# Merged turns of a decoder kernel: row maxima ahead of the eviction of the projections, and the feed-forward's products ahead of turned scores and head outputs

## What is computed

```
h = _layernorm(x, ln1_s, ln1_b)
q, k, v = h @ Wq + bq, h @ Wk + bk, h @ Wv + bv
qp = elu(q) + 1.0;  kp = elu(k) + 1.0
kv = einsum('bshd,bshm->bhmd', kp, v);  ksum = sum(kp, axis=1)
z = 1.0 / (einsum('blhd,bhd->blh', qp, ksum) + EPS_ATTN)
x = x + (einsum('blhd,bhmd,blh->blhm', qp, kv, z) @ Wo + bo)
x = x + relu(_layernorm(x, ln2_s, ln2_b) @ W1 + b1) @ W2 + b2
```

```
scores = einsum('bhqd,bhkd->bhqk', q, k) / sqrt(D_HEAD)
_, idx = top_k(scores, TOP_K)
attn = einsum('bhqk,bhkd->bhqd', softmax(where(kept, scores, -inf)), v)
return x + attn @ w_out_w.T + w_out_b
```

## Time and profile before

| | us |
|---|---|
| median of 3 runs | 1457.76 |
| lowest and highest | 1451.19, 1458.03 |
| the profiled execution | 1452.29 |
| its span | 1450.5 |
| TensorE busy, share of the span | 1045.4, 72% |
| VectorE | 998.1, 69% |
| ScalarE | 670.8, 46% |
| GpSimd | 478.6, 33% |

### The profile page before, as it was taken

The page is one execution under the profiler, slowest core; times in us unless marked ns, Lnnn a source line. Parts: engine busy times, 40 slices in busy tenths (PEclk is TensorE's granted clock), DMA queues, the critical chain, the costliest instruction groups (busy, mean ns, idle before and its releaser), DMA issues.

```text
span 1450.5 us, 17894 instructions
## 1 busy us (share of the span) xinstructions
PE 1045.4 (72%) x5082; PEld 692.4 (48%) x5082; DVE 998.1 (69%) x3106; ACT 670.8 (46%) x1767; POOL 478.6 (33%) x468
## 2 busy tenths in 40 slices
PE   3887764555466727777584669878899883988999
PEld 2676642323244515555362334333344452766787
DVE  5666668878547778777876876753867858765332
ACT  2444425733166515665413754335776653633322
POOL 4233335602244413444522730033433423221100
PEclk9989976866677858887655889989999895889999
DMA  4100010000000000000001001101111120222343
GB/s 124 30 13 25 29 50 0 1 0 1 0 13 17 14 1 26 5 17 9 1 1 51 1 1 53 50 22 48 51 45 45 47 74 15 74 70 92 113 136 122
DMA packets 41106, 53.88 MB, mean 37 GB/s; under 512 B 6112, under 2 KB 20080, under 8 KB 41008
## 3 DMA queue, kind: packets, MB, share of 16 engines
q1 hardware_dynamic: 40336, 50.80, 11.5%
q0 software_dynamic: 672, 1.98, 0.4%
HBM read 51.71 MB, written 1.05 MB: 36 GB/s over the span
## 4 chain that ended last, share of the span: by engine, by line
PE 42%; DVE 24%; ACT 7%; issue 6%; POOL 5%; DVEq 1%; POOLq 0%; ACTq 0%
PE psum L1663 7%; PE psum L1674 6%; PE psum L1649 6%; PE psum L1406 2%; PE psum L1430 2%; PE psum L1524 2%; PE psum L1388 2%; POOL Wk L680 2%; PE psum L1336 2%; PE psum L1258 2%; PE psum L1478 2%; DVE S L2461 2%; DVE smax L2466 2%; ACT far L988 2%; DVE nmax L2045 1%
## 5 line engine op out<-in xcount | busy, mean ns | idle before, releaser
L2173 DVE TENSOR_TENSOR big<-psum,qe 128x512 f32<-128x512 f32 x106 | 72.9, 688 | 157.5 <-PE psum L1674 75.5
L1134 ACT ACTIVATE qe<-psum 128x512 f32<-128x512 f32 x106 | 62.3, 595 | 127.6 <-PE psum L1663 127.5
L1649 PE MATMUL psum<-big,wexp 128*128 128x256 f32 (+1 forms) x340 | 117.8, 462 | 0.0
L988 ACT ACTIVATE far<-far,half_far,fmul 128x128 bf16<-128x128 bf16 x256 | 102.9, 488 | 22.5 <-DVE hit L1948 22.5
L637 POOL TENSOR_SCALAR veps<-mv 128x4 f32<-128x4 f32 x34 | 8.3, 244 | 291.0 <-DVE mv L1868 291.0
L1961 DVE MAX8 near<-Wk 128x8 f32<-128x128 f32 x512 | 103.0, 275 | 0.0
L735 POOL TENSOR_TENSOR Wk<-Wk,far 128x1024 f32<-128x1024 f32 x32 | 68.2, 2134 | 67.2 <-ACT far L988 67.2
L1258 PE MATMUL psum<-ident,h 128*128 128x128 f32 x172 | 37.5, 347 | 71.0 <-DVE h L1875 47.7
L1649 PEld LDWEIGHTS psum<-big,wexp 128*128 128x128 f32 x340 | 70.0, 206 | 30.5 <-issue 21.9
L1875 DVE TENSOR_SCALAR h<-xs,mv,rstd 128x128 f32<-128x128 f32 x128 | 53.1, 478 | 41.3 <-POOL rstd L639 38.1
L1336 PE MATMUL psum<-ident,Wk 128*128 128x128 f32 x256 | 45.7, 344 | 49.1 <-POOL Wk L680 45.4
(11 more groups left out here) (344 smaller groups left out, 2898.2 us busy)
## 6 DMA issues: line engine op xcount, KB each, us to landing
wexp<-in_mg SPq DMA_DIRECT2D x48, 256.0 KB, 2.6
wexp<-in_mu SPq DMA_DIRECT2D x48, 256.0 KB, 2.9
wexp<-in_md SPq DMA_DIRECT2D x48, 256.0 KB, 3.0
w<-in_aw SPq DMA_DIRECT2D x8, 256.0 KB, 2.9
w<-in_w2a SPq DMA_DIRECT2D x8, 256.0 KB, 2.5
wqkv<-in_aw SPq DMA_DIRECT2D x8, 192.0 KB, 2.2
ctxt<-in_ctx SPq DMA_DIRECT2D x5, 256.0 KB, 5.2
xin<-in_x SPq DMA_DIRECT2D x4, 256.0 KB, 3.0
```

The source lines that it names most:

```text
L988: ins = act.activation(far[t][:, hd, :], far[t][:, hd, :], ACT.Identity, bias=half_far[:, 0:1], scale=fmul[t][:, hd:hd + 1])
L1649: mm = pe.matmul(bank(4)[:, 0:w], wd[l % 2][:, c + j, :], hid_of[k >= EARLY][k % CH][:, j * w:(j + 1) * w], start=first and j == 0, stop=l ...
L2173: dve.tensor_tensor(hid_of[k >= EARLY][k % CH], bank(U_BANK[k]), sg_of[k >= EARLY][k % 2], ALU.mult).then_inc(hu_done, 1)
```

## The change

Four engines have a `merged_turn`; three of them are rewritten, in order alone. No instruction is added or taken away.

- DVE: `maxima(b)` stood between the unsettled check of `b - 1` and its branch; it now stands ahead of `head_outputs` and of the eviction of the projections.
- PE: `turned_maxima` ahead of `sums`; `feed(b, 0)` ahead of the first half of the turned scores; `feed(b, 1)` ahead of the second half; the first two quads of head outputs behind `down`, the last two behind `output`.
- ACT: the copy of the feed-forward's input ahead of the spread maxima; the first two hidden chunks ahead of the first exponential.

```
@@ ACT, merged_turn @@
+                if fed:
+                    feed(b, "input")
                 if 0 <= b - 1 < NB:
                     maxima(b - 1)
-                if fed:
-                    feed(b, "input")
                 if here:
                     penalties(b, range(0, 6))
+                if fed:
+                    feed(b, 0)
                 if old:
                     exponentials(b - 2, 0)
-                if fed:
-                    feed(b, 0)
                 if here:
                     penalties(b, range(6, 11))
                 if old:
@@ PE, merged_turn @@
                     feed(b, "input")
+                if before:
+                    turned_maxima(b - 1)
                 if step:
                     attend(b + 1, "sums")
-                if before:
-                    turned_maxima(b - 1)
+                if fed:
+                    feed(b, 0)
                 if old:
                     turned_scores(b - 2, 0)
-                if fed:
-                    feed(b, 0)
                 if step:
                     attend(b + 1, "attention")
-                if old:
-                    turned_scores(b - 2, 1)
                 if fed:
                     feed(b, 1)
                 if old:
-                    outputs(b - 2, 0)
-                    outputs(b - 2, 1)
+                    turned_scores(b - 2, 1)
                 if step:
                     attend(b + 1, "attended")
                 if fed:
                     feed(b, "down")
                 if old:
+                    outputs(b - 2, 0)
+                    outputs(b - 2, 1)
+                if step:
+                    attend(b + 1, "output")
+                if old:
                     outputs(b - 2, 2)
                     outputs(b - 2, 3)
-                if step:
-                    attend(b + 1, "output")
@@ DVE, merged_turn @@
                     step_normalize("F", b + 1)
+                if here:
+                    maxima(b)
                 if old:
                     head_outputs(b - 2)
                 if after:
                     attend(b + 2, "projections")
                 if before:
                     unsettled_rows(b - 1)
-                if here:
-                    maxima(b)
-                if before:
                     settle(b - 1)
```

## The result

The changed kernel took 1476.95 us (median of 4 runs, 1475.96 to 1481.94) against 1457.89 for the kernel before, measured beside it: a ratio of **1.0149, 95% interval 1.0126 to 1.0173**, some 22 us slower by that ratio (19 between the medians). The profiled execution took 1477.58 us with a span of 1475.8, against 1452.29 and 1450.5; the second is one of the shorter ones of the kernel before, so the 25.3 us between the two spans are more than the measured loss. The forecast was 1461 and its range ended at 1472: the direction of its sum was right, its size was not.

What follows compares the result with a forecast made beforehand. No engine is full in a turn; a chain across engines, mainly VectorE and TensorE, bounds it. Turn 1's 1.4 plus 5 x 1.0 gave +6.4 us on 1454.6, so 1461 us, range 1448 to 1472.

Steps and rivals of the forecast that it cites:

- Early maxima, bare branch: Row maxima moved ahead of the eviction leave the settled branch bare (some 1.55 us); keys come 0.73 earlier, at +4.10.
- Hold by GpSimd: GpSimd's product starts earlier, beside VectorE's queries in turns 2 to 6, holding them near 4 us; masked sums end at +12.62.
- the value for turn 1: In turn 1 the keys are held by GpSimd's product: +1.4 us, between -1.4 and +2.4, the latter if queries late too.
- Head outputs behind `down`, 1.69: On TensorE, 1.69 us of head outputs comes after down, ahead of output projection and scores, in turns 2 to 6.
- The clock is worth 0.2 here, not 1.8: Ahead of attention in turns 2 to 6: a higher clock ends turned scores at +10.99, but attention waits for masked sums, +12.62.
- So I charge nothing for the clock: The gap ahead of down, two pieces under 1 us, shorter than the 1.31 before the second scores, costs no clock.
- a sign of a falling clock: Down products taking well above 4 us, over 5 instead of 3.57, would show the clock falling ahead of them.
- The rival of a clock falling in the new gap: Clock falls in the wait ahead of down: up to 2.0 us in five turns, +16.4 in all, 1471; chance 0.24.

Runs made afterwards that it cites:

- e3: The changed kernel, but GpSimd starts its product of scores and signs only when the positive queries are done: 1462.89 us, ratio 1.0050 to the kernel before.
- e13: The kernel before, with two groups of head outputs (narrow products) computed a second time behind down in turns 2 to 6: 1486.10 us, ratio 1.0197.
- e14: The kernel before, with eight wide 128x128 products added behind down in turns 2 to 6: 1473.53 us, ratio 1.0115.
- e9: The changed kernel, with the first two groups of head outputs also computed ahead of down, filling TensorE's idle time: 1482.19 us, ratio 1.0153 to the kernel before.
- e7: The changed kernel with the edits of e3, e4 and e5 together: 1440.75 us, ratio 0.9895 to the kernel before.
- e4: The changed kernel, but ScalarE evicts up products 2 and 3 ahead of the second exponential: 1469.09 us, ratio 1.0095 to the kernel before.
- e5: The changed kernel with the move of the head outputs undone, the first two groups again ahead of down: 1455.16 us, ratio 0.9998 to the kernel before.
- e6: The changed kernel with the edits of e3 and e4 together: 1447.48 us, ratio 0.9953 to the kernel before.

## Why the prediction was wrong

By its own steps:

- *Early maxima, bare branch: right.* Forecast keys at +4.10, measured +3.82 in turn 4, where the branch showed 1.24 bare, not 1.55; in turn 2 it showed 1.89 and the keys came at +4.48.
- *Hold by GpSimd: right, and the value for turn 1 too small.* L2267 took 4.09 in turn 4, masked sums ended at +12.34 (forecast +12.62); with GpSimd's product behind the queries (e3) it took 0.68. The Trainium skill (SBUF — State Buffer, SBUF: two separate sides) has the ports that the two engines share as an exclusive lock, and the trace agrees: the held queries ended 0.54 behind GpSimd's product. In turn 1 the forecast was +1.4 with a bound of +2.4. Keys and queries were both held (3.16 and 1.75), which made `at` 2.3 late and the turn 3.3 longer; e13 and e14, which change nothing in turn 1, had 34.62 and 35.01 there, so between 2.2 and 3.3 of it is the change. The bound, not the value, was near.
- *Head outputs behind `down`, 1.69: right.* From the start of `down` to first scores it took 8.11 in turn 4 against 6.34 before.
- *"The clock is worth 0.2 here, not 1.8": wrong.* I had let TensorE arrive early, wait for the masked sums and then go on at the upper level. In turn 4 it waited 3.23 and then took 4.56 for attention and the second up products instead of 2.75; `down` started at +21.30, 1.5 behind the forecast +19.80, which the clock's 1.8 covers. e3 takes the wait away, and there the same products take 2.85 in turn 4. I had given the clock its worth where it rises, and not asked what the wait that it makes does next.
- *"So I charge nothing for the clock": wrong, and the step that failed.* I had compared the gap ahead of `down` with one of 1.31 that left no mark, and taken for granted that only idle time counts. In the changed kernel that same 1.31 is followed by 2.07 or 2.08 in turns 2, 3, 5 and 6, and `down`, which I had put at 3.57 and whose passing 4 I had named as a sign of a falling clock, takes 5.44 and 5.47 in turns 2 and 3. Turns 2 and 3 lost 1.7 in `down` and 0.95 in the second scores, turns 4 to 6 1.8 behind the wait for attention, turn 5 another 0.95, turn 6 another 0.4 in the first scores. That is some 12 of the 22.8 us in the table, on a clock that I had charged nothing for. In five turns the forecast was +1.0 each, measured +3.0 to +4.3. What the runs put in its place: 2.5 per turn for a longer run of narrow products (e13 against e14), and for short gaps either nothing or 1.6 in `down`, undecided.

The rival of a clock falling in the new gap was the nearest (1471 against 1477). It had a part of the mechanism, and put it ahead of `down` alone; that its time came near is partly luck, for only in turns 2 and 3 did the clock fall there. It should have had more than 0.24. The Trainium skill (TensorE: Matmul & The Clock Gate, HAM oscillation) names idle gaps as what takes the clock down; the rows of e9 and e13 show a fall with no gap, behind narrow products, where the rule taken alone would have left it at the upper level.

The 1.6 in turns -1 and 0 can't be put down to the change: e14 leaves these turns as they were and took 32.05 in turn 0, the kernel before 30.58.

So the change holds a gain that the forecast did not look for: early maxima and early up products with all three side effects mended are worth 1.1% (e7). The change as made paid for them with head outputs on the path to the scores and with a lower clock. That a longer run of narrow products lowers it is shown (e13, e14), and that the wait of 3.2 ahead of attention goes with a fall which goes when the wait does (e3). That in the changed kernel the two groups of head outputs lower it by standing close together is argued, not shown.

## What to carry to other kernels

Before moving a group of small products off a gap, ask what fills the gap then, and what clock the work behind it will get: the filler here was worth more than its own length. Where the rows show the level falling behind a run of narrow products, try parting it by wide ones. And when a change loses, mend its side effects one by one and together before dropping it: by itself none of e3, e4 and e5 beat the kernel before, two of them together did (e6, 0.5%), and all three did better (e7, 1.1%).

## What the runs showed of the hardware

A run of 16 products of 128x10 (32 records), 3.9 us without a gap on record, took TensorE from its upper level (2.4 GHz) to its lower (1.2 GHz): the output projection behind it took 2.05 instead of 1.14 and the first scores 2.08 instead of 1.13 (e13, turn 4). With the first 8 of them replaced by 8 products of 128x128 of about the same length (1.8 against 1.7) the level stayed (e14). I had not expected busy time to do that.
